# A four-layer perceiver on one core: order of copies and turns in the self attentions, earlier weight loads in layer 2's experts, one product moved in layer 1's scan

## The chip, the cores and the metric

The kernel runs on one core of a Trainium2 chip. The core has TensorE (matmuls and transposes, here called turns), VectorE, ScalarE, GpSimd, a queue that issues DMAs (SyncE) and 16 DMA engines. The metric is the time of one execution in microseconds (us). TensorE runs at one of two clock levels, 1.2 and 2.4 GHz; the profile prints the granted clock as a share of the full one.

## What is computed

Twelve sublayers run on 512 tokens (8 sequences of 64) of 512 features, in four layers of cross attention, self attention (or a scan) and experts. The change touches four of them:

```python
x = x + _L0_attn_ref(_layernorm(x, axis=-1), L0_attn_w_qkv, L0_attn_w_proj)
...
x = x + _L1_attn_ref(_layernorm(x, axis=-1), L1_attn_in_proj_W, ...)
...
x = x + _L2_attn_ref(_layernorm(x, axis=-1), L2_attn_ln1_g, ...)
x = x + _L2_ffn_ref(_layernorm(x, axis=-1), L2_ffn_Wg, L2_ffn_W1, L2_ffn_W2)
...
x = x + _L3_attn_ref(_layernorm(x, axis=-1), L3_attn_Wq, ...)
```

A self attention, the form in layer 2 (two such blocks in a row, each with its own MLP):

```python
att = jnp.einsum('bhqd,bhkd->bhqk', q, k) * scale
att = jnp.where(allowed[None, None], att, neg_inf)
att = jax.nn.softmax(att, axis=-1)
y = jnp.einsum('bhqk,bhkd->bhqd', att, v)
x = x + y @ wo[i] + bo[i]
```

Layer 1's second sublayer is a scan over the 64 steps, whose states are then multiplied by a query and gated:

```python
xs = (jnp.swapaxes(A11, 0, 1), jnp.swapaxes(A12, 0, 1), jnp.swapaxes(beta, 0, 1), jnp.swapaxes(Kh, 0, 1), jnp.swapaxes(Vg, 0, 1))
_, Y = jax.lax.scan(step, S0, xs)
y = jnp.sum(Q * Y, -1).reshape(b, s, DI)
...
y = y * jax.nn.silu(z)
return residual + y @ out_W.T
```

Layer 2's experts: each token goes to one of eight, each of which has 8 places per sequence:

```python
h = jax.nn.gelu(jnp.einsum('becd,edh->bech', expert_inputs, W1))
expert_outputs = jnp.einsum('bech,ehd->becd', h, W2)
```

## The kernel before

All tokens stay in on-chip memory as four tiles (`T = 4`) of 128 rows. Each stage is a block: every engine has its own instruction list, written out by hand in program order, with waits on semaphores between engines, and at a block's end all engines meet. So an engine never works past a block boundary, while DMAs that were issued may.

**Self attention** (`attention`, four uses: layer 0, layer 2 twice, layer 3). Per tile `t` of 128 tokens (two sequences) TensorE does `scores(t)` for 16 heads; VectorE subtracts the maximum (`centre`); ScalarE takes the exponential of all heads at once (`power(t)`, 128x1024). TensorE turns the result in two halves, `turn_probs(t, 0)` and `turn_probs(t, 1)`, both through bank 4, so the second half waits until ScalarE has copied the first out of it (`take_turned(t, g)`, signal `turned_taken`). `attend(t)` multiplies by the values, VectorE divides (`normalise_output`), `turn_output(t)` turns the output, ScalarE copies it (`take_output`), and `project(t)` multiplies by the output weights. `turn_output(0)` begins with idle matmuls (`run_idle`, 12 in layer 0, where `custom` is set, and 8 elsewhere), whose results nobody reads. ScalarE's list in L1420 to L1433 is one row of such steps; an exponential that stands ahead of a copy delays it.

**Layer 1's scan** is two blocks. In `L1_states` VectorE runs 63 dependent steps; meanwhile TensorE does "filler" products that the next block needs (`Fillers`, units 0 to 31, of which 16 to 31 are the query products, each 8 matmuls of 128x512), up to unit `LATE`, and ScalarE copies each out of its bank. Weights for a filler come in four slots; a load waits until the product four jobs back is done. `L1_outputs` begins with 20 idle matmuls, does `outputs(c)` for the 8 chunks (it spreads two rows of factors over the heads, two banks per chunk, in turns), with the remaining filler units between, then the gate products `gates(n)`, and between these a small product with the mean matrix (L3730) once VectorE has summed `y`. VectorE's chunk `c` (L3779 to L3783) waits for `outputs(c)`.

**Layer 2's experts** (`L2_ffn`) go in four pairs. A pair takes 16 loads of 1 MiB: `W1` of either expert in four parts `g`, `W2` likewise. `up(p, g)` for both experts, gelu, turn, `down(p, g)`, then VectorE copies the pair's output (L2994). `first` holds `W1` of a pair's first expert, `second` of the other; a part is loaded again once `up` of the pair before has read it. The first expert's four parts are sent in the stage before (`L2_last_tokens`), all other loads within `L2_ffn`. `L2_xattn_and_attn` keeps its own `qT`, `w`, `w2` (1 MiB each).

## Time and profile before

| | us |
|---|---|
| median of three runs | 3475.48 |
| lowest, highest | 3473.3, 3480.61 |
| the profiled execution | 3483.41 |
| its span, first to last instruction | 3481.7 |

| engine | busy us | share of the span |
|---|---|---|
| TensorE, matmuls | 3141.4 | 90% |
| VectorE | 1225.4 | 35% |
| ScalarE | 711.3 | 20% |
| GpSimd | 392.2 | 11% |

The mean granted TensorE clock is 0.954. The share of busy time is a mean over stages with different limits: layer 3's experts at the end are a stream of 1 MiB weight loads at about 420 GB/s, and the earlier stages depend on TensorE, VectorE or both. A change is to be read at its place, by the wait that ends last there. Matmuls in fp32 stand as two records each, so `x16` in a row of the trace is 8 matmuls of the code.

### The profile page before, as it was taken

The page shows a single profiled execution, that of the slowest core. Times are in us where ns is not written, and L with a number is a line of the kernel's source. Part 1 is how long each engine was busy: PE and PEld are TensorE (multiplying, and loading weights), DVE is VectorE, ACT ScalarE, POOL GpSimd, SP SyncE. Part 2 cuts the span into 40 slices and gives each one's busy share as a digit, 9 for nine tenths or more (in the row PEclk, how much of TensorE's full clock was granted, in tenths as well). Part 3 has the DMA queues.
Part 4 walks back from the last instruction along what each step waited for, and adds up shares of the span by engine and source line. Part 5 has one row for each costly group of instructions (what it writes and reads, how often), then busy time and mean ns, then how long its engine had stood idle before and what let it go on. Part 6 is the DMA issues. An engine that isn't in the chain of part 4 may idle for free. (4 is left out here: it accounts for less than half of the span.)

```text
span 3481.7 us, 44924 instructions
## 1 busy us (share of the span) xinstructions
PE 3141.4 (90%) x18285; PEld 1729.3 (50%) x18285; DVE 1225.4 (35%) x2569; ACT 711.3 (20%) x1365; POOL 392.2 (11%) x386
## 2 busy tenths in 40 slices
PE   9999899998999999999899999989999997666666
PEld 6776653434444544444567675436886752111111
DVE  3675520002444579765341132113555320000000
ACT  2443101101332331111112120003442201000000
POOL 4442010001000000001000000004441000000000
PEclk9999999999999999999999999999999999788887
DMA  2102189997111212220530111981102169999998
GB/s 106 46 33 77 47 332 410 417 417 324 73 48 48 76 37 67 91 89 33 232 156 25 57 74 63 422 345 51 37 13 108 55 242 409 420 419 420 420 420 353
DMA packets 104220, 653.77 MB, mean 188 GB/s; under 512 B 20216, under 2 KB 29433, under 8 KB 41209
## 3 DMA queue, kind: packets, MB, share of 16 engines
q1 hardware_dynamic: 99360, 637.67, 45.5%
q0 software_dynamic: 4160, 13.63, 1.0%
q8 instruction: 121, 1.98, 0.2%
q14 instruction: 43, 0.35, 0.0%
q10 hardware_dynamic: 536, 0.14, 0.0%
HBM read 641.89 MB, written 9.50 MB: 187 GB/s over the span
## 5 line engine op out<-in xcount | busy, mean ns | idle before, releaser
L3103 PE MATMUL banks<-ring,h 128*32 128x512 f32 x1024 | 168.6, 767 | 81.6 <-DMA ring<-in_L_ffn_w 56.8
L3086 PE MATMUL banks<-ring,mine 128*32 128x512 f32 x1024 | 165.9, 697 | 54.1 <-DMA ring<-in_L_ffn_w 53.7
L924 PE MATMUL banks<-ring 128*128 128x256 f32 x784 | 179.9, 381 | 0.0
L1861 PE MATMUL banks<-ring,xT 128*64 128x512 f32 x736 | 166.3, 606 | 14.6 <-DMA ring<-in_L_ffn_Wu 6.8
L509 PE MATMUL banks<-normed_features,first 128*128 128x256 f32 x768 | 167.2, 379 | 0.4 <-ACT normed_features L476 0.4
L3214 DVE COPY mine<-mT 128x32 f32<-128x32 f32 x31 | 5.6, 181 | 448.0 <-PE banks L3086 448.0
L924 PEld LDWEIGHTS banks<-ring 128*128 128x128 f32 x784 | 144.5, 190 | 28.7 <-issue 11.4
L509 PEld LDWEIGHTS banks<-normed_features,first 128*128 128x128 f32 x768 | 145.3, 190 | 21.6 <-issue 2.0
L434 POOL TENSOR_TENSOR rstd_pairs<-var_eps_pairs,minus_half 128x4 f32<-128x4 f32 x30 | 30.9, 1030 | 1104.5 <-DVE var_eps_pairs L422 929.4
L150 PE MATMUL banks<-identity 128*128 128x128 f32 x780 | 111.0, 307 | 18.6 <-PEq L142 18.6
L3103 PEld LDWEIGHTS banks<-ring,h 128*32 128x32 f32 x1024 | 26.5, 123 | 196.0 <-DMA ring<-in_L_ffn_w 145.2
L150 PEld LDWEIGHTS banks<-identity 128*128 128x128 f32 x780 | 107.0, 222 | 27.8 <-issue 27.5
L1861 PEld LDWEIGHTS banks<-ring,xT 128*64 128x64 f32 x736 | 60.3, 140 | 117.2 <-issue 116.0
L897 PE MATMUL banks<-big 128*128 128x512 f32 x256 | 117.0, 601 | 0.0
L3086 PEld LDWEIGHTS banks<-ring,mine 128*32 128x32 f32 x1024 | 34.3, 117 | 164.3 <-DMA ring<-in_L_ffn_w 113.2
L893 PE MATMUL banks<-big 128*128 128x512 f32 x256 | 113.1, 595 | 1.0 <-ACT big L1067 1.0
L3352 PE MATMUL banks<-big,ring 128*128 128x512 f32 x256 | 111.5, 595 | 0.0
L2062 DVE TENSOR_TENSOR h<-banks,sg 128x512 f32<-128x512 f32 x23 | 15.9, 692 | 243.2 <-PE banks L1861 243.2
L509 PE MATMUL banks<-normed_features,ring 128*128 128x256 f32 x448 | 97.7, 379 | 2.1 <-DMA bo<-in_L_xattn_bo 1.7
L1886 PE MATMUL banks<-ring,hT 128*64 128x512 f32 x368 | 88.4, 615 | 12.1 <-DMA ring<-in_L_ffn_Wd 6.7
L509 PEld LDWEIGHTS banks<-normed_features,ring 128*128 128x128 f32 x448 | 84.6, 190 | 14.6 <-DMA bo<-in_L_xattn_bo 2.0
L3352 PEld LDWEIGHTS banks<-big,ring 128*128 128x128 f32 x256 | 48.1, 190 | 62.9 <-issue 62.9
(660 smaller groups left out, 5291.9 us busy)
## 6 DMA issues: line engine op xcount, KB each, us to landing
ring<-in_L_ffn_w SPq DMA_DIRECT2D x256, 1024.0 KB, 27.1
ring<-in_L_ffn_Wd SPq DMA_DIRECT2D x24, 2048.0 KB, 21.7
ring<-in_L_ffn_Wg SPq DMA_DIRECT2D x23, 2048.0 KB, 24.3
ring<-in_L_ffn_Wu SPq DMA_DIRECT2D x23, 2048.0 KB, 21.6
wb<-in_L_ffn_W SPq DMA_DIRECT2D x32, 1024.0 KB, 25.0
first<-in_L_ffn_W SPq DMA_DIRECT2D x16, 1024.0 KB, 20.9
second<-in_L_ffn_W SPq DMA_DIRECT2D x16, 1024.0 KB, 23.1
ctxT<-in_ctxT SPq DMA_DIRECT2D x8, 1024.0 KB, 5.0
```

The costliest lines, as they stand in the source:

```text
L150: pe.matmul(m.ps[:, bank, 0:P], m.ident[:], m.ident[:], start=True, stop=True)
L434: pool.tensor_tensor(m.rstd2[:, 2 * half:2 * half + 2, :].rearrange("p t i -> p (t i)"), m.den2[:, 2 * half:2 * half + 2, :].rearrange("p ...
L509: ins = pe.matmul(m.ps[:, self.banks[q % R], 0:256], w[:, k, mm * P:(mm + 1) * P], m.yT[:, k, 256 * half:256 * half + 256], start=(k == 0) ...
L893: ins = pe.matmul(ps[:, u % 2, :], wkb[:, k, u * P:(u + 1) * P], (extraT if knorm else ctxT[:, par])[:, k, :], start=(k == 0), stop=(k == ...
L897: ins = pe.matmul(ps[:, u % 2, :], ctxT[:, par, k, r * P:(r + 1) * P], wvb[:, k, :], start=(k == 0), stop=(k == C - 1))
L924: ins = pe.matmul(halves(n % 2)[:, r, :], a, x, start=(k == 0), stop=(k == 1))
L1861: ins = pe.matmul(ps[H * side:H * side + H, 2 * kind + half, :], xT[:, p % 2, k, H * own:H * own + H], rows_of(where[(name, slot)], C)[:, ...
L1886: ins = pe.matmul(ps[H * side:H * side + H, 6, :], part, rows_of(where[("Wd", slot)], FC)[:, k, :], start=(k == 0), stop=(k == FC - 1))
L2062: dve.tensor_tensor(h[:, HALF * half:HALF * half + HALF], ps[:, 2 + half, :], sg[:, half, :], ALU.mult)\
L3086: ins = pe.matmul(ps[B4 * q:B4 * q + B4, 0, :], mine[:, e % 2, k, :], w[:, q * 512:(q + 1) * 512], start=(k == 0), stop=(k == C - 1))
L3103: ins = pe.matmul(ps[B4 * q:B4 * q + B4, 2, :], h[:, Q * n + q, :], w[:, q * D:(q + 1) * D], start=(n == 0), stop=(n == Q - 1))
L3352: ins = pe.matmul(bank, self.slot(f, 8)[:, k, :], self.u[:, k, :], start=(k == 0), stop=(k == 7))
```

## The change

It has three parts.

1. Self attentions. ScalarE's exponential of tile 2 is moved behind both copies of tile 1. On TensorE `scores(3)` and `turn_probs(1, 0)` are taken out of the loop and ahead of it, and in the loop `turn_probs(t + 2, 0)` stands between `attend(t + 1)` and `project(t)`, where before both halves stood side by side behind `project`.
2. Layer 2. Three of the four parts of `W1` of the second expert are sent in the stage before, into a buffer `second` that now exists for the whole layer; the layer's attention keeps its `w`, `w2` and `qT` in it. The fourth part has a buffer of its own, `fourth`, and is sent first in `L2_ffn`.
3. Layer 1. One more filler unit (and its load) moves from `L1_outputs` to `L1_states`; the 20 idle matmuls at the start of `L1_outputs` go; the last two `outputs` stand behind the first and the second gate product.

```diff
@@ attention, TensorE
             attend(0)
+            turn_probs(1, 0)
+            scores(T - 1)
             for t in range(T - 1):
-                turn_probs(t + 1, 0)
-                if t + 3 < T:
-                    scores(t + 3)
                 turn_probs(t + 1, 1)
                 turn_output(t)
                 attend(t + 1)
+                if t + 2 < T:
+                    turn_probs(t + 2, 0)
                 project(t)
@@ attention, ScalarE
             take_turned(0, 1)
-            power(2)
             for t in range(T - 1):
                 take_turned(t + 1, 0)
                 take_turned(t + 1, 1)
+                if t == 0:
+                    power(2)
                 take_output(t)
@@ L2_xattn_and_attn
-    with m.local(qT=[P, C, N], w=[P, C, D], w2=[P, C, D], b=[P, 2, C], bv=[P, D],
-                 ctx=[P, 2, 2, KC, D]) as (qT, w, w2, b, bv, ctx):
+    w, w2, qT = (second[:, i] for i in range(3))
+    with m.local(b=[P, 2, C], bv=[P, D], ctx=[P, 2, 2, KC, D]) as (b, bv, ctx):
@@ L2_layer, loads sent in L2_last_tokens
-            *[(w1_landed[0][g], (first[:, g], d["L2_ffn_W1"][0, g])) for g in range(4)]])
+            *[(w1_landed[0][g], (first[:, g], d["L2_ffn_W1"][0, g])) for g in range(4)],
+            *[(w1_landed[1][g], (second[:, g], d["L2_ffn_W1"][1, g])) for g in range(3)]])
@@ L2_ffn
-        wa = (first, second)
+        wa = [[first[:, g] for g in range(4)], [*(held[:, g] for g in range(3)), fourth[:]]]
...
-            for g in range(4):
-                load_up(0, 1, g)
+            load_up(0, 1, 3)
...
-                pe.wait_ge(*w1_landed[1][g].at(16 * p + 16))
+                pe.wait_ge(*w1_landed[1][g].at(16 * p + (0 if g < 3 else 16)))
@@ L1_states
-    EARLY, LATE = 6, F[8] + 13
+    EARLY, LATE = 6, F[8] + 14
...
-            for _ in range(fill.SLOTS, 8 + 13 + 2):
+            for _ in range(fill.SLOTS, 8 + 14 + 2):
@@ L1_outputs
-    left, last = fill.first_unit[8] + 13, len(fill.units)
+    left, last = fill.first_unit[8] + 14, len(fill.units)
...
-            run_idle(m, pe, 4, 20)
             outputs(0)
             outputs(1)
...
             for n in range(NC):
                 gates(n)
+                if n < 2:
+                    outputs(NC - 2 + n)
```

TensorE's list in layer 0's attention, from `attend(0)` (L1341, L1348) on; L1326 is `turn_probs`, L1304 `scores`, L1363 `turn_output`, L1371 `project`. Before:

```order
L1326 MATMUL banks<-identity,sc 128x128 x4
L1304 MATMUL banks<-ctxT,qT 64x64 x32
L1326 MATMUL banks<-identity,sc 128x128 x4
L150 MATMUL banks<-identity 128x128 x12
L1363 MATMUL banks<-identity,o 128x128 x4
L1341 MATMUL banks<-v,prT 64x32 x32
L1348 MATMUL banks<-v,ones_rows 64x256 x4
L1371 MATMUL banks<-w,oT 128x512 x4
L1326 MATMUL banks<-identity,sc 128x128 x8
L1363 MATMUL banks<-identity,o 128x128 x4
```

The same stretch now:

```order
L1326 MATMUL banks<-identity,sc 128x128 x4
L1304 MATMUL banks<-ctxT,qT 64x64 x32
L1326 MATMUL banks<-identity,sc 128x128 x4
L150 MATMUL banks<-identity 128x128 x12
L1363 MATMUL banks<-identity,o 128x128 x4
L1341 MATMUL banks<-v,prT 64x32 x32
L1348 MATMUL banks<-v,ones_rows 64x256 x4
L1326 MATMUL banks<-identity,sc 128x128 x4
L1371 MATMUL banks<-w,oT 128x512 x4
L1326 MATMUL banks<-identity,sc 128x128 x4
L1363 MATMUL banks<-identity,o 128x128 x4
```

The row of eight turns (two halves of a tile) is split: four stand ahead of the output product, four behind it. Up to the first `turn_output` TensorE's order is the same.

ScalarE's list in the same attention; the first rows are the exponentials (L1420, then L1421), `take_turned` (L1426, then L1427) and `take_output` (L1433, then L1434). Before:

```order
L1420 ACTIVATE sc<-sc 128x1024 x2
L1426 ACTIVATE prT<-banks 128x512 x2
L1420 ACTIVATE sc<-sc 128x1024
L1426 ACTIVATE prT<-banks 128x512 x2
L1433 ACTIVATE oT<-banks 128x512
L1426 ACTIVATE prT<-banks 128x512 x2
```

And now:

```order
L1421 ACTIVATE sc<-sc 128x1024 x2
L1427 ACTIVATE prT<-banks 128x512 x4
L1421 ACTIVATE sc<-sc 128x1024
L1434 ACTIVATE oT<-banks 128x512
L1427 ACTIVATE prT<-banks 128x512 x2
```

The third exponential stood between the two pairs of copies and now stands behind both.

TensorE's list around the boundary between `L1_states` and `L1_outputs`; the `big,ring` rows are filler products of 8 matmuls each, `quantT,sel` is `outputs`, `normed_features,big` the gates, `tmp,mean` the mean. Before:

```order
L3352 MATMUL banks<-big,ring 128x512 x88
L142 UNCONDITIONAL_BRANCH
L3684 UNCONDITIONAL_BRANCH
L150 MATMUL banks<-identity 128x128 x20
L3691 MATMUL banks<-quantT,sel 128x512 x4
L3352 MATMUL banks<-big,ring 128x512 x8
...
L3352 MATMUL banks<-big,ring 128x512 x8
L3691 MATMUL banks<-quantT,sel 128x512 x4
L3701 MATMUL banks<-normed_features,big 128x512 x16
L3730 MATMUL banks<-tmp,mean 128x64
...
L150 MATMUL banks<-identity 128x128 x20
L3708 MATMUL banks<-big 128x512 x32
```

And now:

```order
L3354 MATMUL banks<-big,ring 128x512 x96
L142 UNCONDITIONAL_BRANCH
L3686 UNCONDITIONAL_BRANCH
L3693 MATMUL banks<-quantT,sel 128x512 x4
L3354 MATMUL banks<-big,ring 128x512 x8
...
L3693 MATMUL banks<-quantT,sel 128x512 x4
L3703 MATMUL banks<-normed_features,big 128x512 x4
L3693 MATMUL banks<-quantT,sel 128x512 x2
L3703 MATMUL banks<-normed_features,big 128x512 x4
L3693 MATMUL banks<-quantT,sel 128x512 x2
L3703 MATMUL banks<-normed_features,big 128x512 x8
L3733 MATMUL banks<-tmp,mean 128x64
```

The scan's block has 96 filler matmuls in its last row where it had 88, the next block two products in place of three, no idle row at its start, and its last four spread matmuls stand behind the first two gates.

## Rows read from the trace of the kernel before

**Rows 1.** Timeline, layer 0: start us, duration us, engine, line, operation [idle before].

```profile
388.15 0.91 PE L1304 MATMUL banks<-ctxT,qT 32*64 32x64 f32 x64 [0.54 <-DVE sc L1479]
...
391.61 0.58 ACT L1426 ACTIVATE prT<-banks 128x512 f32<-128x512 f32 x1
391.96 0.69 DVE L1524 TENSOR_TENSOR o<-mix,col 128x512 f32<-128x512 f32 x1
...
392.24 1.12 PE L1326 MATMUL banks<-identity,sc 128*128 128x128 f32 x4 [3.18 <-ACT prT L1426]
...
393.15 4.71 PE L150 MATMUL banks<-identity 128*128 128x128 f32 x24
...
397.69 0.60 PE L1363 MATMUL banks<-identity,o 128*128 128x128 f32 x4
```

**Rows 2.** Windows: length, busy of PE, PEld, DVE, ACT, POOL, PEclk, DMA share, GB/s.

```profile
389.00:392.20 3.20, 0.06 (x5) 0.00 (x0) 3.10 (x5) 1.54 (x2) 0.00 (x0) 0.69 0.02 5
...
1822.00:1823.50 1.50, 1.50 (x7) 1.50 (x8) 1.50 (x3) 0.37 (x1) 0.00 (x0) 0.50 0.10 44
```

**Rows 3.** Timeline, layer 0, tile 2: halves side by side, `attend(2)`, last exponential.

```profile
404.57 0.66 PE L1326 MATMUL banks<-identity,sc 128*128 128x128 f32 x4 [0.69 <-ACT prT L1426]
...
405.92 1.14 PE L1341 MATMUL banks<-v,prT 64*64 64x32 f32 x64 [0.25 <-ACT prT L1426]
406.24 1.06 ACT L1420 ACTIVATE sc<-sc 128x1024 f32<-128x1024 f32 x1
```

**Rows 4.** Timeline, first attention of layer 2: `scores(3)`, output ready, its turn.

```profile
1817.97 0.91 PE L1304 MATMUL banks<-qkh 32*64 32x64 f32 x64
...
1820.56 0.69 DVE L1530 TENSOR_TENSOR o<-banks,col 128x512 f32<-128x512 f32 x1
...
1826.30 1.06 PE L1363 MATMUL banks<-identity,o 128*128 128x128 f32 x4
```

**Rows 5.** Timeline, second attention of layer 2: the same stretch.

```profile
2013.37 0.91 PE L1304 MATMUL banks<-qkh 32*64 32x64 f32 x64
...
2018.88 0.80 PE L1326 MATMUL banks<-identity,sc 128*128 128x128 f32 x3 [1.16 <-issue]
...
2022.37 0.60 PE L1363 MATMUL banks<-identity,o 128*128 128x128 f32 x4
```

**Rows 6.** Timeline, layer 3's attention: the second half's turn, the idle matmuls.

```profile
2715.36 0.66 PE L1326 MATMUL banks<-identity,ring 128*128 128x128 f32 x4 [0.72 <-ACT ring L1426]
...
2715.85 1.95 PE L150 MATMUL banks<-identity 128*128 128x128 f32 x16
```

**Rows 7.** Timeline, layer 1: end of the scan, and the block behind it.

```profile
1340.10 75.80 PE L3352 MATMUL banks<-big,ring 128*128 128x512 f32 x176
1420.91 0.29 DVE L3651 TENSOR_TENSOR big<-big,normed_tokens 128x128 f32<-128x128 f32 x1
1421.73 7.63 PE L150 MATMUL banks<-identity 128*128 128x128 f32 x40 [5.83 <-PEq L142]
...
1457.48 1.23 DVE L3779 TENSOR_TENSOR tmp<-banks,big 128x1024 f32<-128x1024 f32 x1 [2.53 <-PE banks L3691]
1458.15 14.00 PE L3701 MATMUL banks<-normed_features,big 128*128 128x512 f32 x32
...
1463.97 5.06 DVE L3791 TENSOR_TENSOR big<-big 128x2048 f32<-128x2048 f32 x5
...
1472.36 4.49 DVE L3806 TENSOR_TENSOR big<-big,banks 128x2048 f32<-128x2048 f32 x2 [3.07 <-PE banks L3730]
```

**Rows 8.** Layer 2's experts: VectorE's pair outputs, TensorE's last wait, a window.

```profile
2221.74 0.69 DVE L2994 COPY o<-banks 128x512 f32<-128x512 f32 x1 [13.20 <-PE banks L2888]
2255.30 0.69 DVE L2994 COPY o<-banks 128x512 f32<-128x512 f32 x1 [13.20 <-PE banks L2888]
...
2325.99 3.65 PE L2888 MATMUL banks<-wb,hT 128*64 128x512 f32 x16 [1.27 <-DMA wb<-in_L_ffn_W]
2329.69 0.69 DVE L2994 COPY o<-banks 128x512 f32<-128x512 f32 x1 [14.72 <-PE banks L2888]
...
2260.00:2280.00 20.00, 20.00 (x90) 7.50 (x88) 2.77 (x4) 1.79 (x3) 0.00 (x0) 1.00 1.01 422
```

More of the change, by code:

```diff
@@ L2429, in _, with L2_xattn_and_attn @@
             norm_output(3, 7 * T)
-def L2_xattn_and_attn(m, first, gw, gate_sent, disp, next_loads):
+def L2_xattn_and_attn(m, first, second, gw, gate_sent, disp, next_loads):
     d = m.d
@@ L2826, in L2_ffn @@
     down_done, o_taken, combined = s("switch_down"), s("switch_o_taken"), s("switch_combined")
-    with m.local(xT=[P, C, E, SL], cmbT=[P, PAIRS, N], second=[P, 4, C, 512], wb=[P, 2, 4, 4, D], hq=[P, 2, 512], hT=[P, 4, 512],
+    with m.local(xT=[P, C, E, SL], cmbT=[P, PAIRS, N], fourth=[P, C, 512], wb=[P, 2, 4, 4, D], hq=[P, 2, 512], hT=[P, 4, 512],
                  o=[P, 2, D], sc=[P, T, E], top=[P, T], gate=[P, T], cmp=[P, T * E, E], eq=[P, T, E], one=[P, T, E],
                  hot=[P, T * E, CAP]) as \
-            (xT, cmbT, second, wb, hq, hT, o, sc, top, gate, cmp, eq, one, hot), m.block() as block:
+            (xT, cmbT, fourth, wb, hq, hT, o, sc, top, gate, cmp, eq, one, hot), m.block() as block:
         ps = m.ps
-        wa = (first, second)
+        wa = [[first[:, g] for g in range(4)], [*(held[:, g] for g in range(3)), fourth[:]]]
         @block.sync
@@ L2866, in up @@
                     for i in range(2):
-                        ins = pe.matmul(ps[HALF * i:HALF * i + HALF, g % 2, :], xT[:, k, 2 * p + i, :], wa[i][:, g, k, :],
+                        ins = pe.matmul(ps[HALF * i:HALF * i + HALF, g % 2, :], xT[:, k, 2 * p + i, :], wa[i][g][:, k, :],
                                         start=(k == 0), stop=(k == C - 1))
```

12 lines of the change are left out of this document (6 added, 6 removed).

## The prediction, made before the changed kernel ran

> **What bounds the kernel now.** One core works through its stages in a row, each closed by a block boundary at which all engines meet, so time taken out of one stage moves all that follows, weight loads included. I read, in this order, the slices of the page (TensorE busy nearly everywhere; the DMA engines full in layer 0's and layer 2's experts and from the first load of layer 3's experts to the end), then the timeline of each place that the diff touches, then the windows with granted clock and GB/s. The chain of waits is nearly all layer 3's weight loads; these start at a block boundary, so a shift ahead of them comes through to the end. There are three kinds of place.
>
> In the self attentions TensorE waits once for ScalarE. In layer 0, `scores(3)` ends at 389.06; the turn of the next tile's second half starts at 392.24, because it waits for a copy that ScalarE gives at 391.61, behind the exponential of tile 2 [rows 1]. Then come the 12 idle matmuls (4.71 us), and the output's turn starts at 397.69, though VectorE had the output ready at 392.65. The granted clock says why the idle ones are slow: during the 3.2 us of waiting it fell to a mean of 0.69, and behind the same wait in layer 2 it was 0.50, the 1.2 GHz level [rows 2]. At the full clock 16 such records take 1.95 us [rows 6]: 0.12 us each, not 0.20.
>
> At the end of layer 1's scan TensorE has been out of work for 5.83 us, then does 7.63 us of idle matmuls at the lower level, while VectorE waits for the first spread outputs [rows 7]. From there TensorE carries the path up to the gates.
>
> In layer 2's experts the two loads per step are always queued. VectorE's copy of a pair's output comes 33.56 us after the one before where weights never wait, but the last two together take 74.39 us [rows 8]: 74.39 - 67.12 = 7.27 us of waiting for weights.
>
> **Attentions: copies ahead of the exponential.** The wait ahead of the second half's turn goes; the turn then follows `scores(3)` directly. What is late next is the slower of the idle matmuls and the output.
> Layer 0: 389.06 + 0.66 (turn) + 24 x 0.12 (idle) = 392.6; the output is ready at 392.65. The output's turn starts at 392.7 in place of 397.69: **5.0 us** [rows 1, 6].
> Layer 2, first: `scores(3)` ends at 1818.88, + 0.66 + 1.95 = 1821.5; output ready at 1821.25. Turn at 1821.5 in place of 1826.30: 4.8; the turn itself takes 1.06 at the low clock and 0.60 at the full one, + 0.5: **5.3 us** [rows 1, 4].
> Layer 2, second: ends at 2014.28, + 2.6 = 2016.9 in place of 2022.37: 5.5. But here one turn is split by 1.16 us in which TensorE lacked an instruction [rows 5]; weights were streaming, and I leave that stall in: **4.3 us** (bounds 1.2, if the instructions come no earlier than 2018.88 whatever the order, and 5.5).
> Layer 3 waits only 0.72 us: **0.7 us** [rows 6].
>
> **Attentions: turns split around the output product.** Twice in each attention the second half's turn waits 0.69 us for the copy of the first, as the two stand side by side [rows 3]. With `project` between them that copy is long done: 2 x 0.69 = 1.4. The turn of the last tile's first half now stands right behind `attend(2)`, and the last exponential is still running: before, `attend(2)` starts at 405.92 with 1.14 us of records, and the exponential goes from 406.24 to 407.30 [rows 3]. VectorE, on whose result that exponential depends, isn't moved by the change, and TensorE comes 0.7 earlier. I take a new wait of 0.4 (bounds 0 and the whole exponential, 1.06); `project(1)` is queued behind it. Net **1.0 us** each, 4.0 in all. The exponential of tile 2 standing two copies later costs nothing: its reader now comes behind `attend(1)`. VectorE keeps its order and, by my count of its instructions between two attended tiles, stays just within TensorE's shortened turn; rival 5 is the case where it doesn't.
> Sum: 5.0 + 5.3 + 4.3 + 0.7 + 4.0 = **19.3 us**.
>
> **Layer 1: one product more under the scan, no idle matmuls, two outputs among the gates.** A product is 75.80 / 11 = 6.9 us. TensorE ends at 1415.90 + 6.9 = 1422.8 instead, ScalarE's copy of it (0.6) at 1423.4, 2.2 us behind the scan's end at 1421.20; the boundary takes 0.5 (1421.20 to 1421.73), so the next block starts at 1423.9, at the full clock [rows 7]. Before, it works from 1429.36 to 1458.15 on three products and four pairs of outputs: 28.8 - 20.7 = 8.1, 2.0 a pair. Now: 3 pairs (6.0), 2 products (13.9), a gate (3.5), an output (1.0), a gate (3.5), the last output (1.0): 1452.8. VectorE needs 3.2 us for a chunk (two from 1457.48 to 1463.97) and is just free: 1456.1; then its sum over steps, to 1461.4 (5.06 and a last small piece of 0.2), and the mean at 1461.8. TensorE has its four gates done at 1423.9 + 28.9 + 7.0 = 1459.8, and waits 1.6 us for VectorE: the bound changes engines here. Before, VectorE takes the mean at 1472.36: **10.6 us**. Behind it all engines stand as before. The moved load of the last weights waits for a product that now has four others (28 us) ahead of the one that needs them, and the `z` weights, sent at the block's start, are wanted 20 us into it: nothing. Bounds: 7 (a clock lost in the 1.6 us) and 11.
>
> What the idle matmuls were for is shown by the trace: after 5.83 us without work the clock was at the 1.2 GHz level. What is left of that gap now is 1.1 us. The Trainium skill ("TensorE: Matmul & The Clock Gate", The HAM clock gate) says that an idle TensorE is throttled to half rate and that activity releases it, a rule that speaks against taking fillers away; the drop behind the gap agrees with it. By it alone the first real work could run at half the clock, and the gain here would be some 3 us smaller.
>
> **Layer 2: three parts of the second expert early.** 3 MiB go out of the stage's queue into the one before, where nothing else is loading once the first expert's 4 MiB are in. At 422 GB/s they are 7.45 us [rows 8]. The buffers are those of that layer's own query and output weights and normed tokens, free by then. Weights last made TensorE wait until 2325.99; 7.45 earlier is 2318.5, + 3.65 for the last down product = 2322.2. TensorE without any wait would be there at 2329.69 - 7.27 = 2322.4. The two ends meet: **7.2 us**, bounds 5.5 and 7.3. The queue doesn't run dry: it holds 9 MiB at the start, 22 us, and the first reload waits only for the pair's first up product, which comes a little before that.
>
> **Sum.** 19.3 + 10.6 + 7.2 = 37.1 us. Against the profiled execution's 3483.4 that is 3446.3; the median of the runs is 3475.5, from which I take 37.1 off: **3438 us**, 1.1% faster.
>
> **Rivals.** (1) *The low clock stays.* In layer 0 the clock fell although TensorE had been idle for only 3.2 us, behind small matmuls. If it still falls in the attentions of layers 0 and 2, their idle matmuls cost 0.08 more a record, 24 x 0.08 + 2 x 16 x 0.08 = 4.5, and in layer 1 the new 1.6 us wait costs up to 3: some 7 us, 3445. For it: three of four attentions show it. Against: layer 3, with a wait of 0.72, kept its clock, and the waits now are that short.
> (2) *Layer 2's weights bring nothing*, as TensorE's own work or a dry queue bounds there: 3445. Against: the 7.27 us are seen.
> (3) *TensorE lacks instructions* in the second attention of layer 2, and also in the first, as both run beside 8 MiB of weights: -3.1 and up to -4: 3442 to 3445.
> (4) *Slower.* The 1.6 us wait ahead of layer 1's mean drops TensorE to 1.2 GHz, and it stays there through the four gates and the output products, whose waits for VectorE keep it low. Four gates are 14.0 us [rows 7] and the output product has twice as many matmuls of that size, 28: 42 us that would double, against a gain of 37: 3480. It decides only if the low level lasts over 37 us; the low stretch in the rows here ended within 7.6 us, under dense work.
> (5) *It doesn't do what it says:* VectorE's chain binds the attentions all the same, which leaves 18 to 20 of the 37 us: 3457.
>
> **Chances.** Forecast 0.62, rival 1 0.15, rival 2 0.07, rival 3 0.08, rival 5 0.06, rival 4 0.02. The sums of the bounds reach from 3475.5 - 44 to 3475.5 - 24, and the medians themselves lie within 7 us; the range is 3430 to 3451, with rivals 1 to 3 inside. About 0.2% (7 us) is what a measurement of this kernel can tell from no change: faster by more 0.95, within it 0.03, slower 0.02.
>
> **What would show it.** In the changed profile: no wait for a copy ahead of the turn behind `scores(3)`, and a granted clock of 1.00 there; the output's turn about 5 us earlier in three attentions and under 1 us in layer 3; no wait for the copy of a first half, but a short one for the exponential once per attention; in layer 1 about 1.1 us between the last product and the first output, and the mean 38 us behind the block's start in place of 51; layer 2's pair outputs 33.6 us apart throughout. I am wrong if the low clock is still there, if pairs 3 and 4 still take longer, or if VectorE's chunk in layer 1 comes later than 1456 less the earlier shifts.

## The result, and the profile after

The changed kernel takes **3440.74 us** (median of 4 runs, 3438.37 to 3443.76) against 3477.93 beside it: ratio 0.9901, 95% interval 0.9888 to 0.9914, which is 34 us less (30 to 39); the plain difference of the two medians is 37. Two later comparisons gave 0.9899 (0.9878 to 0.9919) and 0.9908 (0.9893 to 0.9922).

The profiled execution after has a span of 3436.7 us against 3481.7, 45 us less. That is more than the runs say, and it can be seen where the surplus sits: the length of a stage is read from SP's first DMA issue in it to the first of the next, and stages that the change doesn't touch differ too. The stretch up to layer 0's attention went from 367.42 to 362.91 us, and layer 0's experts, 422.54 before, were between 415.0 and 424.0 in the profiles of all later runs. So I compare stage by stage, and use three profiles of the changed kernel.

Timeline of the DMA issues, kernel after: start, duration, queue, line, operation. These two rows are the two ends of layer 0's attention (before: 367.42 and 424.66).

```profile
362.91 0.33 SPq L177 DMA_DIRECT2D w<-in_L_attn_w_proj  x1
413.91 0.60 SPq L177 DMA_DIRECT2D ring<-in_L_ffn_Wg  x1
```

| stage, us | before | after, three profiles | predicted | measured (mean) |
|---|---|---|---|---|
| layer 0, attention | 57.24 | 51.00, 51.00, 50.99 | -6.0 | -6.2 |
| layer 1, scan | 222.48 | 223.81, 223.71, 223.77 | +2.2 | +1.3 |
| layer 1, outputs | 108.91 | 97.52, 97.51, 97.51 | -12.7 | -11.4 |
| layer 2, first attention | 109.94 | 105.06, 104.13, 105.05 | -6.3 | -5.2 |
| layer 2, second attention | 110.14 | 108.67, 104.70, 105.26 | -5.3 | -3.9 |
| layer 2, experts | 162.26 | 154.87, 154.78, 154.78 | -7.2 | -7.4 |
| layer 3, attention | 114.26 | 112.00, 112.51, 112.59 | -1.7 | -1.9 |
| sum | | | -37.0 | -34.8 |

The sum of the stages, 34.8, agrees with the 34 of the ratio. One mark is skewed: in the profile before, SP's first issue in layer 1's outputs' block comes at 1422.39, as its last filler load ran until 1422.34, while TensorE is at work there from 1421.73; in the changed kernel the two stand 0.04 us apart. Counted from TensorE's first matmul the scan grew by 2.0 and the outputs' block shrank by 12.1; their sum is the same. The five rows other than layer 2's attentions came in within 1.3 us of the prediction; layer 2's second attention is the only row that differs much between executions.

**Layer 0's attention**, timeline of TensorE after, the stretch that answers to [rows 1], and its windows (length; busy PE, PEld, DVE, ACT, POOL; PEclk, the granted clock; DMA share; GB/s).

```profile
383.64 1.02 PE L1304 MATMUL banks<-ctxT,qT 32*64 32x64 f32 x64 [0.53 <-DVE sc L1481]
384.59 0.66 PE L1326 MATMUL banks<-identity,sc 128*128 128x128 f32 x4
385.08 2.84 PE L150 MATMUL banks<-identity 128*128 128x128 f32 x24
388.20 0.66 PE L1363 MATMUL banks<-identity,o 128*128 128x128 f32 x4 [0.28 <-DVE o L1526]
```

```profile
384.00:385.50 1.50, 1.50 (x60) 1.43 (x58) 1.47 (x2) 0.22 (x1) 0.00 (x0) 1.00 0.04 11
385.50:388.00 2.50, 2.42 (x22) 2.23 (x20) 2.43 (x4) 1.44 (x2) 0.00 (x0) 1.00 0.00 0
```

The wait of 3.18 us ahead of the second half's turn is gone, the 24 idle records take 2.84 us at the full clock where they took 4.71, and the output's turn starts 4.6 us behind the start of `scores(3)`, where it was 9.5. It now waits 0.28 us for VectorE's output: that is the new bound, as the prediction had it.

**Layer 2's second attention**, the same stretch after (before: [rows 5]).

```profile
1985.97 0.66 PE L1326 MATMUL banks<-identity,sc 128*128 128x128 f32 x4
1986.46 1.95 PE L150 MATMUL banks<-identity 128*128 128x128 f32 x16
1988.25 0.60 PE L1363 MATMUL banks<-identity,o 128*128 128x128 f32 x4
1988.78 0.47 PE L1341 MATMUL banks<-v,prT 64*64 64x33 f32 x17
1991.51 1.50 PE L1341 MATMUL banks<-v,prT 64*64 64x33 f32 x47 [2.26 <-issue]
1992.94 1.11 PE L1326 MATMUL banks<-identity,sc 128*128 128x128 f32 x4
1993.85 5.72 PE L1371 MATMUL banks<-second,oT 128*128 128x512 f32 x8
```

The output's turn does come early. But in the middle of `attend(1)`, behind the 17th of its 64 records, TensorE stands still for 2.26 us with nothing that it waits for ("issue"), and what follows runs at the lower level: `project` takes 5.72 us instead of 3.6, and the granted clock from 1993 to 1999.5 is 0.61 on average. Before, the stall was 1.16 us and stood behind the first of the four turns that follow `scores(3)` (a turn of scores or output stands as one record, other matmuls as two). Part of the gain was turned into a longer stall.

**Layer 1**, timeline of the outputs' block, which starts at 1410.18 (TensorE, then VectorE's mean; before: [rows 7]).

```profile
1410.22 1.99 PE L3693 MATMUL banks<-quantT,sel 32*128 32x512 f32 x8 [0.94 <-PEq L142]
1439.47 7.13 PE L3703 MATMUL banks<-normed_features,big 128*128 128x512 f32 x16
1448.28 0.43 PE L3733 MATMUL banks<-tmp,mean 128*128 128x64 f32 x2 [1.68 <-DVE tmp L3794]
1448.75 4.49 DVE L3809 TENSOR_TENSOR big<-big,banks 128x2048 f32<-128x2048 f32 x2 [0.53 <-PE banks L3733]
```

The first spread output stands at the block's start, at full speed (8 records in 1.99 us), and VectorE takes the mean 38.5 us behind TensorE's first matmul of the block, where it was 50.6. TensorE waits 1.68 us for VectorE's sum there.

**Layer 2's experts**, VectorE's pair outputs and TensorE's last wait (before: [rows 8]).

```profile
2286.95 3.65 PE L2890 MATMUL banks<-wb,hT 128*64 128x512 f32 x16 [0.84 <-DMA wb<-in_L_ffn_W]
2290.64 0.69 DVE L2996 COPY o<-banks 128x512 f32<-128x512 f32 x1 [14.26 <-PE banks L2890]
```

The four pair outputs start at 2188.9, 2222.5, 2256.0 and 2290.6: 33.6, 33.5 and 34.6 apart. Only the last still waits for a weight, 0.84 us.

### The profile page after: what moved, and what is told of

Its sections match the earlier page's. It is cut to its first block and busy times, and to the rows that moved or that the text cites. A ratio compares the mean times of both kernels' runs of the same rounds, so it can differ in the third digit from the quotient of the medians.

```text
span 3436.7 us, 44844 instructions
## 1 busy us (share of the span) xinstructions
PE 3113.6 (91%) x18245; PEld 1708.9 (50%) x18245; DVE 1225.3 (36%) x2569; ACT 710.6 (21%) x1365; POOL 391.5 (11%) x386
## 5 line engine op out<-in xcount | busy, mean ns | idle before, releaser
L1863 PE MATMUL banks<-ring,xT 128*64 128x512 f32 x736 | 165.4, 603 | 12.1 <-DMA ring<-in_L_ffn_Wg 6.1
L924 PEld LDWEIGHTS banks<-ring 128*128 128x128 f32 x784 | 144.5, 190 | 28.7 <-issue 11.4
L150 PE MATMUL banks<-identity 128*128 128x128 f32 x740 | 96.4, 290 | 12.7 <-PEq L142 12.7
L150 PEld LDWEIGHTS banks<-identity 128*128 128x128 f32 x740 | 92.2, 204 | 21.1 <-issue 20.8
```

What stands on the lines that cost most here:

```text
L150: pe.matmul(m.ps[:, bank, 0:P], m.ident[:], m.ident[:], start=True, stop=True)
L924: ins = pe.matmul(halves(n % 2)[:, r, :], a, x, start=(k == 0), stop=(k == 1))
L1863: ins = pe.matmul(ps[H * side:H * side + H, 2 * kind + half, :], xT[:, p % 2, k, H * own:H * own + H], rows_of(where[(name, slot)], C)[:, ...
```

## The experiments

The open points were: is the sum made of the parts that I named; does each of the two orders in the attentions bring what I gave it; why layer 2's attentions gave less; and what the idle matmuls do, kept or taken away. All are read by the length of stages; `act_order`, `pe_order`, `hold_w2` and `no_idle` ran once each and have nothing else.

### One part at a time

`attn_only` is the kernel before with the two edits in `attention`:

```diff
             scores(2)
             attend(0)
+            turn_probs(1, 0)
+            scores(T - 1)
             for t in range(T - 1):
-                turn_probs(t + 1, 0)
-                if t + 3 < T:
-                    scores(t + 3)
                 turn_probs(t + 1, 1)
                 turn_output(t)
                 attend(t + 1)
+                if t + 2 < T:
+                    turn_probs(t + 2, 0)
                 project(t)
...
-            power(2)
             for t in range(T - 1):
                 take_turned(t + 1, 0)
                 take_turned(t + 1, 1)
+                if t == 0:
+                    power(2)
```

> Only the self attentions are changed (the copies ahead of the exponential and the split of the turns); layer 1 and layer 2's experts are as before. By the blocks of the changed kernel's trace the four attentions gave 6.2 (layer 0), 4.9 and 1.5 (layer 2), 2.3 (layer 3): 14.9 us, so 0.9957 of the time before. Theory 1, the parts simply add: 3463 us, the second attention of layer 2 again with a stall of about 2 us for instructions. Rival, the stall of that attention came with the phase in which the block meets the weight loads: then it gives up to 5.3 here, and the sum is 18.7 (3459). A gain under 11 us would say that the trace of the changed kernel flattered these blocks.

Measured: 3457.96 us against 3477.22, ratio 0.9945 (0.9924 to 0.9966), which is 19 us (12 to 26). By stages layer 0 gave 6.2 and layer 3 2.3, as expected, but layer 2's attentions gave only 2.6 and 0.6: 11.8 us in all, under the 14.9 that was expected and at the low end of the interval. The total alone would speak for the rival (18.7), but the rival's full gain in layer 2 is not in the stages. In the profile the stage of layer 0's experts was 7.5 us shorter than before with no edit in it; whether that is what the other runs have too, no profile shows. What the stages say is specific: TensorE's timeline in the second attention has the stall again, larger and in another place.

```profile
1992.17 0.91 PE L1304 MATMUL banks<-qkh 32*64 32x64 f32 x64
1993.02 0.33 PE L1326 MATMUL banks<-identity,sc 128*128 128x128 f32 x1
1997.51 0.80 PE L1326 MATMUL banks<-identity,sc 128*128 128x128 f32 x3 [4.16 <-issue]
```

`l1_only` is the kernel before with the edits in layer 1:

```diff
-    EARLY, LATE = 6, F[8] + 13
+    EARLY, LATE = 6, F[8] + 14
...
-    left, last = fill.first_unit[8] + 13, len(fill.units)
+    left, last = fill.first_unit[8] + 14, len(fill.units)
...
-            run_idle(m, pe, 4, 20)
             outputs(0)
...
                 gates(n)
+                if n < 2:
+                    outputs(NC - 2 + n)
```

> Only layer 1 is changed: 14 products under the scan, no idle matmuls at the start of the outputs' block, two outputs among the gates. Theory: the two blocks together are 10.1 us shorter, as in the changed kernel (prediction: 10.6), the clock 1.00 throughout, 3468 us. Rival (a lower clock behind the wait for VectorE at the mean in some executions): under 8 us in the median, though the profile shows 10.

Measured: 3467.65 us, ratio 0.9975 (0.9960 to 0.9990), 9 us. Scan 223.8, outputs 97.5: 10.1 us, the same as in the whole change.

`l2_only` is the kernel before with the edits in layer 2:

```diff
+            *[(w1_landed[1][g], (second[:, g], d["L2_ffn_W1"][1, g])) for g in range(3)]])
...
-            for g in range(4):
-                load_up(0, 1, g)
+            load_up(0, 1, 3)
...
-                pe.wait_ge(*w1_landed[1][g].at(16 * p + 16))
+                pe.wait_ge(*w1_landed[1][g].at(16 * p + (0 if g < 3 else 16)))
```

> Only the three parts of the second expert early. Theory: the experts' block is 7.4 us shorter (162.3 to 154.9), the pair outputs 33.6, 33.6 and 34.6 apart, nothing else moves: 3470.5 us. Rival: the loads that were sent earlier disturb the block before (last tokens, 69.1 us) and give back 1 to 2 us there; then that block is over 70 us.

Measured: 3467.45 us, ratio 0.9972 (0.9960 to 0.9985), 10 us. The experts' block is 154.8 (7.4 less), and the block ahead of it, in which the moved loads now run, 68.7 against 69.1: nothing is given back. The rival falls.

By stages the three parts alone give 11.8 + 10.1 + 7.4 = 29.3 us, the whole 34.8. The difference lies in layer 2's attentions, where `attn_only` gave 3.2 and the changed kernel 9.1 on average; everywhere else the parts add up to within 0.4 us.

### The two orders apart, and the idle matmuls of layer 1

`act_order` is the kernel before with ScalarE's order alone, and in layer 1 only the idle matmuls taken away:

```diff
-            power(2)
             for t in range(T - 1):
                 take_turned(t + 1, 0)
                 take_turned(t + 1, 1)
+                if t == 0:
+                    power(2)
...
-            run_idle(m, pe, 4, 20)
             outputs(0)
```

> Two single edits in stages that don't touch each other, read by the length of the blocks. Attentions: only ScalarE's order is changed (copies ahead of the exponential), TensorE's as before. Theory: this brings the 5.0 us of layer 0 (57.2 to 52.2), about 5.5 in layer 2's first (109.9 to 104.4, more by up to 2 us if TensorE's instructions come late) and 0.7 in layer 3 (114.3 to 113.6); the waits of 0.69 us for the first half's copy stay, twice in each. Rival (VectorE binds as well, so both orders are needed): under 3 us in layer 0. Layer 1: only the 20 idle matmuls at the start of the outputs' block are taken away, 13 products under the scan as before. Theory: the gap of 5.8 us ahead of the block stays, so the first outputs run at a granted clock near 0.5, and the block is 4 to 5 us shorter (108.9 to about 104.5); the rival, that the idle matmuls cost their full 7.6 us, gives 101.3.

Measured: layer 0's attention 52.3 (-4.9), layer 3's 113.5 (-0.7), as expected. Layer 2's gave 3.4 and 3.3, where 5.5 was expected for the first, with issue stalls of 0.79, 1.04 and 1.90 us. Layer 1's outputs' block 106.0, only 2.9 us less for 7.63 us of idle matmuls, where 4 to 5 was expected. The timeline and two windows of its start show where the rest went (TensorE starts at 1407.04).

```profile
1407.04 3.78 PE L3692 MATMUL banks<-quantT,sel 32*128 32x512 f32 x8 [5.83 <-PEq L142]
1410.75 9.46 PE L3353 MATMUL banks<-big,ring 128*128 128x512 f32 x16
...
1422.05 7.13 PE L3353 MATMUL banks<-big,ring 128*128 128x512 f32 x16
```

```profile
1405.00:1412.00 7.00, 4.96 (x10) 2.00 (x11) 4.16 (x8) 0.00 (x0) 0.00 (x0) 0.52 0.53 191
1412.00:1415.00 3.00, 3.00 (x4) 1.11 (x4) 2.90 (x4) 0.00 (x0) 0.00 (x0) 0.50 0.97 415
```

Behind the gap the granted clock is 0.50, the 1.2 GHz level, and the first outputs (3.78 us, 1.99 at the full clock) and the first product (9.46, 7.13 at the full clock) carry what the idle matmuls carried before. Taking them away was worth it only together with the filler product that closes the gap.

`pe_order` is the other half: TensorE's order alone, and layer 1 as changed but with the idle matmuls kept.

```diff
             attend(0)
+            turn_probs(1, 0)
+            scores(T - 1)
...
+                if t + 2 < T:
+                    turn_probs(t + 2, 0)
                 project(t)
...
             run_idle(m, pe, 4, 20)
             outputs(0)
```

> The other halves. Attentions: only TensorE's order is changed, ScalarE's as before. Theory: the wait of about 3 us for the copy behind the exponential stays, and each attention gains about 1.0 us (layer 0 57.2 to 56.2, layer 2's first 109.9 to 108.9, layer 3 114.3 to 113.4). Rival: the exponential ahead of the copy now also holds the turn of the third tile, and the gain is nothing. Layer 1: 14 products and the two outputs among the gates as in the changed kernel, but the 20 idle matmuls kept. Theory: the clock is at 1.00 here, the 40 records take 4.9 us instead of 7.6, and the outputs' block is that much longer than in the changed kernel: 102.4.

Measured: layer 0 56.4 (-0.9), layer 2's first 108.4 (-1.5), layer 3 112.7 (-1.5), outputs' block 102.1. The wait for the copy behind the exponential is there as before, and so is the low clock behind it:

```profile
388.84 1.12 PE L1326 MATMUL banks<-identity,sc 128*128 128x128 f32 x4 [3.18 <-ACT prT L1427]
389.75 5.16 PE L150 MATMUL banks<-identity 128*128 128x128 f32 x24
...
1412.77 4.70 PE L150 MATMUL banks<-identity 128*128 128x128 f32 x40 [0.94 <-PEq L142]
```

In layer 0 and layer 3 the halves add up to the whole (4.9 + 0.9 against 6.2; 0.7 + 1.5 against 2.3), to 0.4 us. The idle matmuls of layer 1, at the full clock, are 4.70 us, and the block is 4.6 us longer than without them: they were pure cost once the gap was closed.

### Why layer 2's attentions gave less

In the three profiles of the changed kernel, in `attn_only`, in `act_order` and in the one stall before, the last stall of each block ends 24.9 to 26.4 us behind the block's start, wherever TensorE had got by then. (`l1_only`, with the attentions as before, has one stall, of 0.80 us in the first, which ends at 19.8 and costs nothing; in `no_idle` they end at 22.4 and 24.4.) In the second attention of the kernel after (block start 1965.16) I laid that beside the DMA traffic: windows (columns as above), then the DMA view of the window 1989 to 1990 (queue: packets, MB, share) and of the block's first 27 us (issue: KB, us from issue to landing).

```profile
1975.00:1985.00 10.00, 10.00 (x198) 6.90 (x194) 5.90 (x11) 2.14 (x3) 0.00 (x0) 1.00 0.99 424
1985.00:1989.00 4.00, 4.00 (x106) 3.65 (x104) 3.93 (x6) 2.36 (x4) 0.00 (x0) 1.00 0.87 377
1989.00:1990.00 1.00, 0.25 (x17) 0.14 (x9) 1.00 (x3) 0.48 (x1) 0.00 (x0) 1.00 0.22 82
1990.00:1991.50 1.50, 0.00 (x0) 0.00 (x0) 0.51 (x1) 0.00 (x0) 0.00 (x0) 0.93 0.00 0
```

```profile
q8 instruction: 1, 0.02, 6.5%
```

```profile
ctx<-in_L_attn_w SPq DMA_DIRECT2D x1, 4096.0 KB, 25.1
```

The 9 MiB sent at the block's start fill the DMA engines for some 24 us. Around the stall one packet of the instruction queue (16 KB) moves, in the window 1989 to 1990, and TensorE resumes at 1991.5. In `attn_only` the packet moves between 1995 and 1996, and TensorE resumes at 1997.5. Looked up in steps of half a microsecond, each of the 19 stalls in layer 2's attentions, over all kernels that have one, ends 2.4 to 3.0 us behind the start of the step in which such a packet moves. The view doesn't name the engine that a packet is for; that these bring TensorE's instructions is inferred from the 19 cases. `hold_loads` takes the traffic away from there: the changed kernel, with the two 4 MiB loads of the feed-forward weights held back until two tiles are attended.

```diff
-        send(block, ahead)
+        if isinstance(ahead, list):
+            @block.sync
+            def _(sp):
+                start_loads(sp, ahead[0:1])
+                sp.wait_ge(*attended.at(2))
+                start_loads(sp, ahead[1:])
+        else:
+            send(block, ahead)
```

> The changed kernel, but in the attentions of layers 2 and 3 the loads of the feed-forward weights (8 MiB) wait until attended tile 2 of 4 is done, so that the dense small matmuls of the first two tiles run without them. Theory A, the weight stream starves TensorE's instruction supply: the stalls of 0.79, 1.04 and 2.26 us fall under 0.2 us each, the low clock behind the last one goes with it; layer 2's first attention block 105.1 to about 103.2, the second 108.7 to about 104.3, some 6 us in all: 3434 us. Rival B, the stalls belong to the place in the code and not to the traffic: they stay, and nothing changes (3440). Rival C, they move with the traffic to the third and fourth tile: same sum, other place.

Measured: 3435.29 us, ratio 0.9890 (0.9866 to 0.9913). Layer 2's attentions are 103.05 and 103.04, and there is no issue stall in either.

```profile
1982.57 1.95 PE L150 MATMUL banks<-identity 128*128 128x128 f32 x16
1984.57 0.66 PE L1370 MATMUL banks<-identity,o 128*128 128x128 f32 x4
1985.15 1.14 PE L1348 MATMUL banks<-v,prT 64*64 64x33 f32 x64
1986.22 0.66 PE L1333 MATMUL banks<-identity,sc 128*128 128x128 f32 x4
...
1986.00:1996.00 10.00, 9.41 (x115) 5.62 (x109) 7.88 (x14) 3.27 (x5) 0.00 (x0) 1.00 0.94 367
1996.00:2006.00 10.00, 9.75 (x100) 5.97 (x99) 5.05 (x11) 3.70 (x8) 1.01 (x1) 1.00 0.97 419
```

The instruction packets, in the same code, now move 14 and 19 us into the block, where they moved at 16 to 17.5 and at 22.5 to 23.5 in the changed kernel: beside the weight stream they are 2 to 4.5 us late. The DMA view of the window 1975 to 1976 has the first of them (the block starts at 1961.57), and SP's timeline the first held load:

```profile
q8 instruction: 1, 0.02, 6.0%
...
1986.35 0.33 SPq L177 DMA_DIRECT2D first<-in_L_attn_w  x1
```

Rival B falls: with the traffic gone the stalls are gone, in the same code. So does rival C: the loads run at 367 and 419 GB/s beside the third and fourth tile, and these don't stall. That the weight traffic causes the stalls is shown; that it does so through the late packet, theory A, rests on the timing of the 19 cases, and no run delays a packet by other means. With the stalls gone the change is worth 6.9 and 7.1 us in these two blocks, where I had forecast 6.3 and 5.3. Against the first profile of the changed kernel the two blocks gained 7.6 us (4.9 against the mean of the three), but the total shows less: the stage ahead of layer 2's attentions was 133.5 us where it was 129.9, and 2.3 us of that are 32 records of one column that took 6.04 us instead of 3.70. That code is the same in both kernels; the low clock stood in that stage in `act_order`, `hold_w2` and `best2` too, and in no other profile. I could not find why, and leave it open.

`hold_w2` holds only the second of the two loads:

```diff
-                start_loads(sp, ahead[0:1])
+                start_loads(sp, ahead[0:2])
                 sp.wait_ge(*attended.at(2))
-                start_loads(sp, ahead[1:])
+                start_loads(sp, ahead[2:])
```

> As hold_loads, but only the second of the two 4 MiB loads waits; the first is sent at the block's start as in the changed kernel. Theory A (an instruction fetch comes back only when the weights queued ahead of it are through): 5 MiB are through some 14 us into the block, before TensorE's dense part at 19 us, so the stalls are gone as in hold_loads and both blocks of layer 2 are at 103.05. Rival: half the traffic leaves half the stalls, and the blocks lie between 103.1 and 105.

Measured: 103.05 and 103.06, no stall. The packets move at 14 and 19 us again. Half of the bytes don't leave half the stall, which fits theory A: what counts by it is whether weights are moving when an instruction packet is due, not how many there are.

### What the idle matmuls in the attentions are for

`no_idle` is the changed kernel with three edits in separate stages:

```diff
                 if t == 0:
-                    run_idle(m, pe, OUT[t], 12 if custom else 8)
+                    pass
...
                 outputs(2 * i + 3)
+            outputs(NC - 2)
+            outputs(NC - 1)
             for n in range(NC):
                 gates(n)
-                if n < 2:
-                    outputs(NC - 2 + n)
...
-            *[(w1_landed[1][g], (second[:, g], d["L2_ffn_W1"][1, g])) for g in range(3)]])
+            *[(w1_landed[1][g], (second[:, g], d["L2_ffn_W1"][1, g])) for g in range(1)]])
```

> Three single edits to the changed kernel in separate stages, read by blocks. Attentions: the idle matmuls ahead of the first output's turn are left out. VectorE's output is ready 0.3 us behind them in layer 0, so they cost nothing as they are; TensorE then stands still for 2.9 us there and about 2 in layer 2. Theory (clock): it falls in that gap as it did before (0.69 over 3.2 us), and layer 0's block grows from 51.0 to 52 to 53; rival: a gap under 3 us leaves the clock at 1.00, and 51.0 stays. Layer 1: outputs 6 and 7 ahead of the gates instead of among them. Expected 97.5 to 98.0 again: TensorE gets to the gates later by what it waits for VectorE's buffers, but the mean waits for VectorE anyway. Rival: the place among the gates was needed, and the block is 3 us longer. Layer 2's experts: only one part of the second expert early instead of three. Theory (each MiB out of the queue is worth its 2.48 us): 154.9 + 4.9 = 159.8; rival (the gain was the earlier start and not the bytes): near 155 or near 162.

Measured: layer 0's attention 53.6 (+2.6), layer 3's 110.5 (-1.6), layer 1's outputs 99.9 (+2.4), layer 2's experts 159.95 (+5.1; 159.8 was expected). Layer 2's attentions lost their idle matmuls too, but with stalls of 2.41 and 4.30 us in them (105.0 and 109.5) they can't be read for that. Timelines of layer 0 and of layer 1, with the window behind layer 0's gap:

```profile
391.02 0.66 PE L1363 MATMUL banks<-identity,o 128*128 128x128 f32 x4 [3.07 <-DVE o L1526]
391.60 1.93 PE L1341 MATMUL banks<-v,prT 64*64 64x32 f32 x64
...
391.00:395.00 4.00, 3.98 (x79) 3.06 (x80) 2.12 (x5) 0.60 (x1) 0.00 (x0) 0.57 0.01 4
```

```profile
1438.74 1.44 PE L3694 MATMUL banks<-quantT,sel 32*128 32x512 f32 x4 [0.54 <-DVE tmp L3783]
1441.98 2.08 PE L3694 MATMUL banks<-quantT,sel 32*128 32x512 f32 x4 [1.80 <-DVE tmp L3783]
1443.99 15.11 PE L3704 MATMUL banks<-normed_features,big 128*128 128x512 f32 x32
```

In layer 0 the gap of 3.07 us is followed by a clock of 0.57: `attend` takes 1.93 us instead of 1.14 and the next `project` 5.13 instead of 3.60. There the idle matmuls pay. In layer 3 VectorE's output is ready when TensorE gets there, so they were in the way. In layer 1 I had missed that behind two short waits (0.54 and 1.80 us) among small matmuls the clock falls too (0.50 from 1440 to 1442): the changed kernel's wait of 1.68 us, behind 8 gate matmuls of 128x512 (16 records), costs only itself. In layer 2's experts one MiB early gives 2.3 us and two more give 5.1: each part counts for its time in the queue, 2.5 us.

### A version that does more

`best1` adds to `hold_loads` an earlier place for layer 1's outputs:

```diff
             outputs(1)
+            outputs(2)
             for i, x in enumerate(range(left, last)):
                 fill.product(pe, x)
-                outputs(2 * i + 2)
                 outputs(2 * i + 3)
+                outputs(2 * i + 4)
             for n in range(NC):
                 gates(n)
-                if n < 2:
-                    outputs(NC - 2 + n)
+                if n == 0:
+                    outputs(NC - 1)
```

> The changed kernel with the feed-forward weights of layers 2 and 3 held until attended tile 2 (as in hold_loads), and in layer 1 the outputs of each chunk one place earlier on TensorE (three ahead of the first product, two behind each product, the last one behind the first gate). Expected against the changed kernel: 2.0 and 5.6 us less in layer 2's attentions as in hold_loads, and 2.2 in layer 1's outputs' block (97.5 to 95.3), because VectorE waits 3.65, 2.61 and 2.52 us for outputs there and the wait of 1.68 us ahead of the mean goes: 9.8 us in all, 3430.5 against 3440. If VectorE isn't what binds there, the block stays at 97.5.

> The changed kernel once more, for a second profile and beside the next one. Expected 3440 us; the attentions' blocks 51.0, 105.1, 108.7 and 112.0 again if the stalls of layer 2 are fixed by the code and the loads and not by chance, the experts' block of layer 2 154.9, the outputs' block of layer 1 97.5.

Measured: `best1` 3432.84 us (0.9889, 0.9868 to 0.9910), `after_again`, the changed kernel beside it, 3438.49 (0.9899, 0.9878 to 0.9919). Its second attention in layer 2 took 104.7, not the 108.7 that fixed stalls would have given: what a stall costs differs between executions. The layer 2 blocks of `best1` are 103.05 both times again. Layer 1's block came out at 96.6, 1.0 less instead of 2.2: the mean starts 37.0 us into the block and now follows the gates directly, so TensorE is the bound from there.

```profile
1436.79 10.57 PE L3710 MATMUL banks<-normed_features,big 128*128 128x512 f32 x24
1447.19 0.33 PE L3741 MATMUL banks<-tmp,mean 128*128 128x64 f32 x2
1447.56 4.49 DVE L3817 TENSOR_TENSOR big<-big,banks 128x2048 f32<-128x2048 f32 x2 [1.08 <-PE banks L3741]
```

`best2` leaves the idle matmuls out in layer 3 alone:

```diff
                 if t == 0:
-                    run_idle(m, pe, OUT[t], 12 if custom else 8)
+                    if not rope:
+                        run_idle(m, pe, OUT[t], 12 if custom else 8)
```

> best1 without the idle matmuls in layer 3's attention alone: without them its block was 110.45 us against 112.0, since VectorE has the output ready there, while in layer 0 the gap that they fill is 3 us and the clock fell behind it, and in layer 2 VectorE ends with them. Expected: layer 3's attention block 110.4 with a granted clock of 1.00, all other blocks as in best1 (103.05 twice in layer 2, 96.5 in layer 1's outputs), in all 1.5 us less than best1, 3431 us. Rival: the gap now falls elsewhere in the attention and the block stays near 112.

> The changed kernel beside best2 on the same chip, a third profile of it. Expected 3439 us; the attention blocks of layer 2 between 103 and 109, by where the instruction fetch falls in this execution, all the others as in the first two profiles (51.0, 97.5, 154.8, 112.0 to 112.5).

Measured: `best2` 3433.6 us (0.9888, 0.9873 to 0.9903), not under `best1`, where 1.5 us less was expected; the changed kernel beside it 3441.38 (0.9908, 0.9893 to 0.9922). Layer 3's block is 110.75, 1.2 less than in `best1`, and layer 2's are 103.04 twice. But layer 1's outputs, the same code as in `best1`, took 98.1 us: the product behind a wait of 0.46 us ran in 8.54 us instead of 7.13.

```profile
1416.46 1.37 PE L3701 MATMUL banks<-quantT,sel 32*128 32x512 f32 x4 [0.46 <-DVE tmp L3791]
1417.76 8.54 PE L3362 MATMUL banks<-big,ring 128*128 128x512 f32 x16
```

So that order puts short waits among small matmuls, and whether the clock holds differs between executions. What stands in every profile that has it (`hold_loads`, `hold_w2`, `best1`, `best2`) is the effect of the held loads on layer 2's attentions; the rest of `best1` and `best2` is about 1 us either way. Their medians lie below the changed kernel's by 5.7 and 7.8 us, but the intervals overlap, so that either is faster than the changed kernel is not shown by the total.

## Why the prediction was right, point by point

**Total.** 3438.0 forecast, 3440.74 measured, within the range; 37.1 us against 34.4 by the ratio. By stages 2.2 us were missing; layer 2's attentions alone fell 2.5 short.

**Copies ahead of the exponential.** Forecast 5.0 in layer 0 and 0.7 in layer 3; `act_order` gave 4.9 and 0.7. The step behind it, that the clock stays up once the wait is gone, holds: 1.00 in the windows, 24 records in 2.84 us. Rival 1 (the low clock stays) falls in layer 0 and layer 3.

**Turns split.** Forecast 1.0 each; `pe_order` gave 0.9, 1.5, 1.4 and 1.5. The new wait for the last exponential, taken as 0.4, is there: 0.52 us in layer 0, 0.30 in the others. Rival 5 (VectorE's chain binds all the same) falls; VectorE's output is the last one ready in layer 0, by 0.28 us.

**Layer 2's attentions, the step that was off.** I left the stall of [rows 5] in at its old size, as if it were a thing of the second attention only, and forecast 5.3 + 1.0 and 4.3 + 1.0. Measured 5.2 and 3.9. The 110.14 of the second block before holds a stall that not every execution has: in `l1_only` and `l2_only` the same code shows none there and takes 109.1 and 109.3, so about 1 us of this block's gain belongs to that one profile. The bound that I had written beside it, "if the instructions come no earlier than 2018.88 whatever the order", comes close to what was found: beside the weights an instruction packet comes 21.5 to 24 us into the block, before the change and after it, and where TensorE stalls it goes on 2.4 to 3.0 us later. Before, the wait for the copy covered that in the first attention, whose packet stands at 22.5 us too and shows no stall; without this wait the stall shows there as well. This is rival 3, to which I gave 0.08 as a case of its own. It holds in part in every execution: against their forecast of 11.6 the two blocks gained 6.4, 11.3 and 9.8 us, and without the traffic 14.0. So the forecast of these two blocks came as near as it did partly by luck: with the copies' wait gone the gain is larger than I had added up, and the stalls, of varying size, took part of it back. `hold_loads` and `hold_w2` show the weight traffic as their cause.

**Layer 1.** Forecast 10.6, measured 10.1. The idle matmuls left, the outputs stand at the block's start, and the wait ahead of the mean is 1.68 us where 1.6 was forecast. Counted from TensorE's first matmul the scan's block grew by 2.0 where 2.2 was forecast, and VectorE's mean comes 12.1 us earlier in the outputs' block where 12.7 was; the sum is 0.5 too large. The scan itself isn't equally long in all executions: with the same 14 products its block was between 220.9 and 223.8 us over ten profiles. But the step from its last operation to the next block, 0.5 us before, was 2.5 in the three profiles of the changed kernel and in `l1_only`, which is the 2.0. Rival 4, that this wait drops the clock for long, falls: the four gates behind it take 13.95 us for 32 records, as at full clock. `no_idle` shows that the mechanism exists in this block all the same, with 1.80 us among small products: +2.4 us. The Trainium skill ("TensorE: Matmul & The Clock Gate", The HAM clock gate) has an idle TensorE throttled; the two waits of nearly one length, of which one cost the clock and one didn't, show that the rule alone doesn't size it here: the rows don't say what else decides.

**Layer 2's experts.** Forecast 7.2, measured 7.4, and 7.4 alone in `l2_only`. The price of a MiB, its time in the queue, holds. `no_idle` gives 5.1 for the last two of the three. The terms differ a little: the last two pair outputs together take 68.2 us instead of 74.4, 6.2 less, as the last pair still waits 0.84 us for a weight; the other 1.2 us came ahead of the first pair's output (47.7 us into the block, 48.8 before), which I had not counted. Rival 2 falls.

**Not forecast.** The block ahead of the experts is shorter, 67.4, 68.7 and 67.4 against 69.1, as its last gate products ran at the full clock (16 records in 1.95 us, 3.58 before) in some executions.

## What to carry to other kernels

When a wait is removed, ask what it covered besides the engine named. Here it also covered a stall that came with a stream of weights, by its timing for a late instruction packet; in this kernel bulk loads that are not needed soon were better sent behind the stretch with the densest small instructions than at the block's start. Idle matmuls were worth their time here only where they filled a gap that would otherwise exist: read each place by itself, since the same line earned 2.6 us in layer 0 and cost 1.6 in layer 3.

## What the runs showed of the hardware that I had not expected

Beside weights at 420 GB/s the 16 KB packets of the instruction queue moved 2 to 4.5 us later than without, and TensorE stood still for 0.4 to 4.3 us, 19 times; each time it went on 2.4 to 3.0 us behind such a packet. In the tiles of `hold_loads` that ran beside the same stream, with products of 128x512 between them, there was no stall. And a wait of 0.46 us between two groups of 32-row matmuls was followed by a product that ran in part at the lower clock level in one execution (8.54 us, a granted clock of 0.67 from 1418 to 1422) and at the full one in another (7.13 us) of the same code.
